# 16-row attentions of a four-layer kernel: negated row maxima turned by VectorE and placed by two small transfers, and maxima run 15 steps ahead

## The chip, the cores and the metric

One Trainium2 chip, one core. The metric is the device time of one execution in microseconds (us); before the change the median of three is 4501.39 us (4497.85 to 4503.6). TensorE (PE, with PEld for its weight loads), VectorE (DVE), ScalarE (ACT), GpSimd (POOL) and SyncE (SP) each work through their own instructions in order and wait for each other on semaphores.

## The reference, cut to what matters

The reference runs four layers, each an attention and a feed-forward part, over x of 8 sequences x 512 rows x 256 columns. The change touches one phase (L0x in the profile) that does three of these parts for all 8 sequences: the attention of layer 0, the gated attention of layer 0 and the attention of layer 1, all with 16 heads of 16 columns. That is 24 items (a part and a sequence each):

```python
qh = (q @ Wq.T + bq).reshape(N, L, h, d)          # h = 16 heads, d = 16
energy = jnp.einsum('nqhd,nkhd->nhqk', qh, kh)
attn = jax.nn.softmax(energy / math.sqrt(d), axis=-1)
out = jnp.einsum('nhql,nlhd->nhqd', attn, vh)
return out @ Wo.T + bo
```

Items 0 to 7 and 16 to 23 are of the kind "cross" (keys and values come from a context), items 8 to 15 of the kind "mixture" (queries are normalised per head, and the result is weighted by gates).

## The kernel before, in words

**Parts in bf16.** float32 queries and keys are cut into three bf16 parts each. GpSimd does this (`split`, lines 373 to 380, four operations of 1024 columns), SP sends the parts to DRAM (`parts_to_scratch`, L313) and loads them back as stacks of six 16-row parts (`stack_rows`, L289): `kstack` and `qstack`, 96 rows, 16 heads, 512 columns, two buffers each. An item needs 12 such loads of 256 KB, and the semaphore `stack_in` counts them.

**Two passes over the scores.** `for_maximum` (L760) multiplies 96 rows of the stacks for a (head, query tile) unit, queries on the partitions, into one of 3 banks of `ps_max`; VectorE takes the row maximum (`maximum`, L485). After 16 units, a group of 4 heads, `negated` (L492, L494) writes minus the maximum as two bf16 parts. `score` (L750) then computes the transposed scores with 104 rows: the 96 of the stacks and 8 more that add minus the maximum, and ScalarE takes the exponential (`exponentials`, L671). `values` (L774) multiplies the exponentials with the values.

**How the maxima get into the rows.** A fill `negmax` of TensorE (L827) multiplies the 128 x 8 block of each query tile with an identity, into the shared bank `ps_t`; ScalarE (`take_negmax`, L684) copies 8 rows x 512 columns for each of 4 heads into `qstack`. As all 4 heads get the same 8 rows, the key rows must pick out a head's own two: `own_key_rows` fills them once.

**Order of the work.** A round has 32 steps and belongs to item q. In step n TensorE does two scores of item q and two maximum units that lie `LEAD` = 12 steps ahead, thus of the next item from step 20 on. Unit 0 of an item waits for all 12 stack loads. After step n with n % 4 = 1 come the values. The other work of TensorE, the fills, goes one at a time through `ps_t` in steps written out by hand in `TURNS`: projections k, q, v, turned copies (xnT, hT, raw, qT), gates and output y, for the items q - 1 to q + 2. VectorE and ScalarE walk through the same steps. `negated` comes in steps 3, 11, 19 and 27, its fill in steps 5, 13, 21 and 29, and the first score of the group in steps 8, 16, 24 and 0.

**SP's queue.** In round q SP waits for the query parts of item q + 1 and stores them, loads kstack, and then

```python
if ahead.there and ahead.cross and ahead.later:
    if nxt.cross:
        sp.wait_ge(taken["v"], nxt.count(2, 2))
    context(ahead)
if nxt.there:
    sp.wait_ge(q_out, nxt.count(16, 16))
    stacked(nxt, 1, q_part, qstack)
```

`context` loads the 512 KB of keys and values of item q + 2 into the one buffer `kv_in`, which the fill v of item q + 1 (steps 9 and 10) reads last. This holds in 13 rounds, 0 to 5 and 15 to 21. The six loads of qstack stand behind it.

**GpSimd's gates.** `split` of the keys of item q + 2 waits for `negmax_ready` of the last group of item q, that of the queries (cross) for the first group of item q + 1.

Of the kernel before, what the change touches and what calls it, by code (L numbers as in the profile page):

```python
# [107 lines left out]
def rounds(steps):  # L108
# [5 lines left out]
    for number in range(-2, ITEMS + 1):  # L114
# [6 lines left out]
    "cross": [(4, "raw", 3), (5, "negmax", 1), (9, "v", 0), (10, "v", 1), (11, "hT", 0), (12, "hT", 1),  # L121
              (13, "negmax", 2), (14, "xnT", 0), (15, "raw", 0), (16, "y", 0), (17, "y", 1), (18, "xnT", 1),
              (19, "k", 0), (20, "k", 1), (21, "negmax", 3), (23, "raw", 1), (24, "q", 0), (26, "q", 1),
              (29, "negmax", 0), (31, "raw", 2)],
    "mixture": [(2, "v", 0), (3, "v", 1), (4, "raw", 3), (5, "negmax", 1), (7, "xnT", 0), (8, "xnT", 1),
                (9, "q", 0), (10, "q", 1), (11, "hT", 0), (12, "hT", 1), (13, "negmax", 2), (14, "k", 0),
                (15, "raw", 0), (16, "k", 1), (18, "gates", 0), (19, "qT", 0), (20, "qT", 1), (21, "negmax", 3),
                (22, "y", 0), (24, "y", 1), (25, "raw", 1), (29, "negmax", 0), (31, "raw", 2)],
# [9 lines left out]
def shift(what, c):  # L138

    if what in ("k", "xnT", "q", "qT"):  # L140
        return 2
    if what == "v" or (what, c) == ("negmax", 0):
        return 1
    if what in ("hT", "gates", "y") or (what, c) == ("raw", 3):
        return -1
    return 0


def softmax_attentions(nc, T, G, name, kind):
# [11 lines left out]
    LEAD = 12  # L161
# [3 lines left out]
    x_sb, ident, identb, own_rows = G["x"], G["ident"], G["identb"], G["own"]  # L165
    with Phase(nc, name) as ph:
# [21 lines left out]
        qstack = [ph.sb(f"qstack{b}", [ROWS + 8, HEADS, S], BF16) for b in range(2)]  # L188
        kstack = [ph.sb(f"kstack{b}", [ROWS + 8, HEADS, S], BF16) for b in range(2)]
        vpad = [ph.sb(f"vpad{b}", [P, TILES, HEADS * (HD + 1) + 15], F32) for b in range(2)]  # L190
        maxes = ph.sb("maxes", [P, TILES, HEADS], F32)
        negmax = ph.sb("negmax", [P, 2, TILES, 4, 2], BF16)
# [34 lines left out]
        vpad_ones, even_own_ready, odd_own_ready = (ph.sem("vpad_ones"), ph.sem("even_own_ready"),  # L227
                                                    ph.sem("odd_own_ready"))
# [51 lines left out]

        def own_key_rows(copy, stack):
            for g in range(4):
                for kt in range(TILES):
                    i = copy(stack[ROWS:ROWS + 8, 4 * g:4 * g + 4, kt * P:(kt + 1) * P], own_rows[ROWS:ROWS + 8])
            return i
# [62 lines left out]
        def _(pool):  # L348
# [84 lines left out]
            bias(Item(0))  # L433
# [2615 lines left out]
```

## Time and profile before

| | us |
|---|---|
| median of three executions | 4501.39 |
| the profiled execution, its time | 4504.13 |
| the profiled execution, its span | 4502.1 |
| first to last score of this phase | 73.9 to 1746.6 |

The times of the rows count from the span's start. Matmul durations in them contain a pipeline's fill and drain, so that two in a row overlap; the distance from start to start is what TensorE spends.

### The profile page before, as it was taken

What the parts mean: (1) busy time and instruction counts of PE and PEld (TensorE: products, weight loads), DVE (VectorE), ACT (ScalarE), POOL (GpSimd) and SP (SyncE); (2) the same over time, 40 slices, a digit from 0 to 9 for tenths busy, and PEclk for the clock granted to TensorE, in tenths of its full rate; (3) what the DMA queues carried; (4) which work ended last, traced back from release to release, by engine and by line L of the source; (5) the groups of instructions that cost most, each with busy time, mean ns of one, the idle gap of its engine ahead of it and who ended that gap; (6) DMA issues with size and microseconds to landing.
All of it is one profiled execution on the core that took longest, in us unless ns stands there. A gap on an engine that the chain in (4) does not pass through costs nothing. (4 is left out here: it accounts for less than half of the span.)

```text
span 4502.1 us, 66443 instructions
## 1 busy us (share of the span) xinstructions
PE 4233.5 (94%) x23716; PEld 2403.0 (53%) x23750; DVE 2976.9 (66%) x7431; ACT 2544.5 (57%) x6408; POOL 810.4 (18%) x550
## 2 busy tenths in 40 slices
PE   6999999999999996778989999999999998999999
PEld 2344344444343343567545666666666665555555
DVE  5767777777767776867675666676776766344333
ACT  3767666666667765633555776767676775111111
POOL 2322444443322311523010000000000000000000
PEclk8999999999999998999999999999999999999999
DMA  8456455444456451000100110010101102000000
GB/s 161 73 76 87 65 63 85 54 69 63 74 75 84 69 71 61 1 15 15 75 12 27 31 32 28 30 36 26 33 27 32 32 27 73 5 5 5 10 5 10
DMA packets 182844, 204.97 MB, mean 46 GB/s; under 512 B 44651, under 2 KB 165099, under 8 KB 180854
## 3 DMA queue, kind: packets, MB, share of 16 engines
q1 hardware_dynamic: 180886, 199.15, 24.1%
q8 instruction: 192, 3.15, 0.3%
q10 hardware_dynamic: 1632, 1.57, 0.3%
q14 instruction: 134, 1.10, 0.1%
HBM read 139.90 MB, written 60.78 MB: 45 GB/s over the span
## 5 line engine op out<-in xcount | busy, mean ns | idle before, releaser
L485 DVE TENSOR_REDUCE L0x_maxes<-L0x_ps_max 128x1 f32<-128x512 f32 x1536 | 976.5, 683 | 291.0 <-PE L0x_ps_max L760 289.3
L671 ACT ACTIVATE L0x_probs<-L0x_ps_sc 128x512 f32<-128x512 f32 x1536 | 822.7, 607 | 362.3 <-PE L0x_ps_sc L750 358.3
L760 PE MATMUL L0x_ps_max<-L0x_kstack,L0x_qstack 96*128 96x512 bf16 x1536 | 588.0, 384 | 22.7 <-DVE L0x_maxes L485 21.3
L2756 ACT ACTIVATE L3x_pexp<-L3x_ps,L3x_nmax 128x77 f32<-128x77 f32 (+2 forms) x1536 | 601.4, 433 | 0.0
L750 PE MATMUL L0x_ps_sc<-L0x_qstack,L0x_kstack 104*128 104x512 bf16 x1536 | 557.7, 384 | 11.5 <-ACT L0x_probs L671 11.0
L2638 DVE TENSOR_REDUCE L3x_nmax<-L3x_ps 128x2 f32<-128x154 f32 (+2 forms) x768 | 346.3, 506 | 242.1 <-PE L3x_ps L2869 239.7
L2764 ACT COPY L3x_pT<-L3x_ps 128x512 f32<-128x512 f32 x512 | 275.1, 593 | 225.8 <-PE L3x_ps L2877 225.4
L2256 ACT ACTIVATE L3f_act_g<-L3f_ps_gu 128x512 f32<-128x512 f32 x128 | 76.4, 597 | 542.2 <-PE L3f_ps_gu L2302 542.1
L774 PE MATMUL L0x_ps_out<-L0x_probs,L0x_vpad 128*32 128x512 f32 x3072 | 371.0, 601 | 1.1 <-ACT L0x_probs L671 1.1
L2654 DVE TENSOR_SCALAR L3x_pexp<-L3x_pexp,L3x_rsum 128x77 f32<-128x77 f32 (+2 forms) x1536 | 357.7, 306 | 6.8
L2756 ACT ACTIVATION_READ_ACCUMULATOR L3x_pexp<-L3x_ps,L3x_nmax 128x1 f32 x1536 | 359.4, 235 | 0.0
L2199 DVE TENSOR_TENSOR L3f_h<-L3f_act_g,L3f_ps_gu 128x512 f32<-128x512 f32 x128 | 88.0, 687 | 383.1 <-ACT L3f_act_g L2256 382.9
L760 PEld LDWEIGHTS L0x_ps_max<-L0x_kstack,L0x_qstack 96*128 96x128 bf16 x1536 | 151.0, 98 | 282.5 <-DVE L0x_maxes L485 167.5
L2895 PE MATMUL L3x_ps<-L3x_pT,L3x_v 128*64 128x128 f32 x4096 | 279.9, 279 | 0.7 <-ACT L3x_oT L2772 0.7
L2877 PEld LDWEIGHTS L3x_ps<-ident,L3x_pexp 128*128 128x128 f32 x2048 | 239.1, 141 | 73.4 <-issue 55.5
L2877 PE MATMUL L3x_ps<-ident,L3x_pexp 128*128 128x128 f32 x2048 | 266.1, 273 | 0.9 <-DVE L3x_pexp L2654 0.9
L750 PEld LDWEIGHTS L0x_ps_sc<-L0x_qstack,L0x_kstack 104*128 104x128 bf16 x1536 | 150.6, 98 | 211.7 <-ACT L0x_probs L671 81.1
L2599 POOL TENSOR_TENSOR L3x_v<-L3x_v,L3x_relv 128x256 f32<-128x256 f32 x32 | 23.4, 731 | 1294.7 <-ACT L3x_v L2739 1294.7
L2302 PE MATMUL L3f_ps_gu<-L3f_xnT,L3f_wg 128*128 128x512 f32 x512 | 243.0, 597 | 2.1 <-DMA L3f_wd<-in_L3f_wd 2.1
L2313 PE MATMUL L3f_ps_y<-L3f_wd,L3f_h 128*128 128x256 f32 x1024 | 242.4, 380 | 1.5 <-DVE x_res L2209 1.5
L2895 PEld LDWEIGHTS L3x_ps<-L3x_pT,L3x_v 128*64 128x64 f32 x4096 | 218.3, 136 | 43.4 <-issue 42.5
L2302 PE MATMUL L3f_ps_gu<-L3f_xnT,L3f_wu 128*128 128x512 f32 x512 | 240.6, 592 | 0.0
(377 smaller groups left out, 6841.4 us busy)
## 6 DMA issues: line engine op xcount, KB each, us to landing
L0x_kstack<-parts_scratch SPq DMA_DIRECT2D x141, 256.0 KB, 10.0
L0x_qstack<-parts_scratch SPq DMA_DIRECT2D x141, 256.0 KB, 14.5
parts_scratch<-L0x_kparts SPq DMA_DIRECT2D x24, 768.0 KB, 3.7
parts_scratch<-L0x_qparts SPq DMA_DIRECT2D x24, 768.0 KB, 5.0
rel_scratch<-L3x_rel_e SPq DMA_DIRECT2D x32, 408.0 KB, 2.4
L3x_rel_d<-prob_scratch SPq DMA_DIRECT2D x32, 408.0 KB, 3.1
L0x_kv_in<-in_ctxT SPq DMA_DIRECT2D x16, 512.0 KB, 4.5
L3x_rel_t<-rel_scratch SPq DMA_DIRECT2D x32, 154.0 KB, 2.4
```

Of the source, the lines that this page charges most:

```text
L485: V.tensor_reduce(maxes[:, t, head:head + 1], ps_max[:, q.count(64, unit) % BANKS, :], AX.X, ALU.max).then_inc(max_taken, 1)
L671: nc.scalar.activation(probs[:, step % SLOTS, j], ps_sc[:, at % BANKS, :], ACT.Exp, scale=HD ** -0.5).then_inc(probs_ready, 1)
L750: nc.tensor.matmul(ps_sc[:, at % BANKS, :], kstack[q.parity][:, head, kt * P:(kt + 1) * P], qstack[q.parity][:, head, :], start=True, stop ...
L760: nc.tensor.matmul(ps_max[:, at % BANKS, :], qstack[q.parity][0:ROWS, head, t * P:(t + 1) * P], kstack[q.parity][0:ROWS, head, :], start=T ...
L774: i = nc.tensor.matmul(ps_out[32 * j:32 * j + 32, :], vpad[q.parity][:, kt, (HD + 1) * head:(HD + 1) * head + 32], probs[:, q.count(STEPS, ...
L2302: i = nc.tensor.matmul(ps_gu[:, n % 2, k], w[:, ci, n * P:(n + 1) * P], xnT[:, ci, :], start=(ci == 0), stop=(ci == C - 1))
L2638: i = V.tensor_reduce(nmax[:, n % 4, s], ps[:, bank:bank + 2, a:b], AX.X, ALU.max, negate=True)
L2654: i = V.tensor_scalar(pexp[:, m % 4, e, a:b], pexp[:, m % 4, e, a:b], rsum[:, m % 4, s, e:e + 1], None, ALU.mult)
L2756: i = nc.scalar.activation(pexp[:, n % 4, e, a:b], ps[:, SB + 2 * (n % 2) + e, a:b], ACT.Exp, bias=nmax[:, n % 4, s, e:e + 1], accum_out=s ...
L2764: nc.scalar.copy(pT[:, m % 2, e], ps[:, TB + e]).then_inc(pt_ready, 1)
L2877: i = nc.tensor.transpose(ps[:, TB + e, kt * P:(kt + 1) * P], pexp[:, m % 4, e, kt * P:(kt + 1) * P], ident[:])
L2895: i = nc.tensor.matmul(ps[DIMH * e:DIMH * (e + 1), OB, at:at + P], v[g % 2][:, vt, h * DIMH:(h + 1) * DIMH], pT[:, m % 2, e, kt * P:(kt + ...
```

## The change

The fill `negmax`, its bank turns and ScalarE's copy go. VectorE lays the two bf16 parts of a group out as 32 columns (head, part, tile), turns them in 32 x 32 blocks into `negT`, ScalarE's queue sends `negT` to DRAM (`negmax_out`, step n % 8 = 1, 8 KB in rows of 64 B) and three steps later, once that has landed, loads them from there into two rows of `qstack`, each head its own (`negmax_in`, step n % 8 = 4, 8 rows of 1 KB). Score rows go from 104 to 98, the two key rows are plain ones set once by a memset, and `LEAD` goes from 12 to 15: `negated` now comes in steps 0, 8, 16 and 24, and unit 0 of the next item in step 17.

```diff
-    "cross": [(4, "raw", 3), (5, "negmax", 1), ... (13, "negmax", 2), ... (21, "negmax", 3), ... (29, "negmax", 0), (31, "raw", 2)],
+    "cross": [(4, "raw", 3), (9, "v", 0), ... (31, "raw", 2)],
...
-    LEAD = 12
+    NEG = 2
+    LEAD = 15
+    OUT_AT, IN_AT = 1, 4
...
-        negmax = ph.sb("negmax", [P, 2, TILES, 4, 2], BF16)
+        negmax = ph.sb("negmax", [P, 2, 4, NEG, TILES], BF16)
+        negT = ph.sb("negT", [P, 2, 32], BF16)
...
+            pool.wait_ge(biased, 1)
+            nc.gpsimd.memset(kstack[1][ROWS:ROWS + NEG], 1.0).then_inc(odd_ones_ready, 1)
+            pool.wait_ge(odd_ones_ready, 1)
...
+            V.memset(kstack[0][ROWS:ROWS + NEG], 1.0).then_inc(even_ones_ready, 1)
...
+                if group >= 2:
+                    dve.wait_ge(neg_turned, group - 1)
...
+                dve.wait_ge(negmax_ready, group + 1)
+                if group >= 2:
+                    dve.wait_ge(neg_out, 16 * (group - 1))
+                V.transpose(negT[:, g % 2, :], negmax[:, g % 2].rearrange("p h e t -> p (h e t)")
+                            ).then_inc(neg_turned, 1)
...
-            def take_negmax(q, g):
-
-                act.wait_ge(in_bank["negmax"], q.count(4, g + 1))
-                nc.scalar.copy(qstack[q.parity][ROWS:ROWS + 8, 4 * g:4 * g + 4, :],
-                               ps_t[ROWS:ROWS + 8, :].unsqueeze(1).broadcast_to([8, 4, S])
-                               ).then_inc(taken["negmax"], 1)
+            def negmax_out(q, g):
+
+                act.wait_ge(neg_turned, q.count(4, g + 1))
+                act.dma_start(T["neg_scratch"].rearrange("x (a r) -> a x r", a=4), negT[:, g % 2, :]
+                              ).then_inc(neg_out, 16)
+
+            def negmax_in(q, g):
+
+                act.wait_ge(neg_out, 16 * q.count(4, g + 1))
+                act.dma_start(qstack[q.parity][ROWS:ROWS + NEG, 4 * g:4 * g + 4, :],
+                              T["neg_scratch"].rearrange("(h e t) p -> e h (t p)", e=NEG, t=TILES)
+                              ).then_inc(neg_in, 16)
...
                     if q.there:
                         exponentials(q, n)
+                    if n % 8 in (OUT_AT, IN_AT):
+                        owner, g = (q, n // 8 + 1) if n < 24 else (q.plus(1), 0)
+                        if owner.there:
+                            (negmax_out if n % 8 == OUT_AT else negmax_in)(owner, g)
...
                 if n % 8 == 0 and j == 0:
-                    pe.wait_ge(taken["negmax"], q.count(4, g + 1))
+                    pe.wait_ge(neg_in, 16 * q.count(4, g + 1))
...
-                elif w == "negmax":
-                    pe.wait_ge(negmax_ready, q.count(4, c + 1))
-                    for t in range(TILES):
-                        i = nc.tensor.matmul(ps_t[ROWS:ROWS + 8, t * P:(t + 1) * P],
-                                             negmax[:, c % 2, t].rearrange("p h e -> p (h e)"), identb[:],
-                                             start=True, stop=True, tile_position=(0, ROWS))
...
+    T["neg_scratch"] = nc.dram_tensor("neg_scratch", (32, P), BF16, kind="Internal").ap()
```

## Rows read from the trace of the kernel before

**Rows 1.** The page: busy time, share of the span and instructions of each engine.
```profile
PE 4233.5 (94%) x23716; PEld 2403.0 (53%) x23750; DVE 2976.9 (66%) x7431; ACT 2544.5 (57%) x6408; POOL 810.4 (18%) x550
```

**Rows 2.** Busy time by stretch: start:end, length, engines, TensorE's clock, DMA share, GB/s.
```profile
74.00:1750.00 1676.00, 1595.30 (x8585) 674.29 (x8583) 1221.33 (x2469) 1128.44 (x1916) 553.33 (x277) 0.99 0.50 70
```

**Rows 3.** Timeline of TensorE around the fill of step 5, round 3.
```profile
284.12 0.38 PE L760 MATMUL L0x_ps_max<-L0x_kstack,L0x_qstack 96*128 96x512 bf16 x1
284.66 0.39 PE L827 MATMUL L0x_ps_t<-identb,L0x_negmax 128*8 128x128 bf16 x4 [0.16 <-DVE L0x_htok L513]
284.98 0.39 PE L750 MATMUL L0x_ps_sc<-L0x_qstack,L0x_kstack 104*128 104x512 bf16 x1
```

**Rows 4.** Groups of instructions, 0 to 2000 us: count, busy, mean ns, idle before.
```profile
L684 ACT CAST L0x_qstack<-L0x_ps_t 8x2048 bf16<-8x2048 f32 x96 | 178.4, 1858 | 15.0 <-PE L0x_ps_t L827 11.8
...
L827 PE MATMUL L0x_ps_t<-identb,L0x_negmax 128*8 128x128 bf16 x384 | 37.0, 218 | 18.5 <-DVE L0x_htok L513 8.6 <-DVE L0x_negmax L494 7.1 <-ACT L0x_qf L698 1.3
```

**Rows 5.** Timeline of SP's queue in round 3, which starts at 276.4 us.
```profile
298.41 0.36 SPq L296 DMA_DIRECT2D L0x_kv_in<-in_ctxT  x1
298.81 2.89 SPq L289 DMA_DIRECT2D L0x_qstack<-parts_scratch  x6
```

**Rows 6.** The six loads of qstack in round 3: their line, 298 to 303 us.
```profile
L289 SPq DMA_DIRECT2D L0x_qstack<-parts_scratch x6: 432/448/449, 298.8 to 301.3; - x6
...
DMA to landing us min/median/max: 6.4/10.9/15.3
```

**Rows 7.** Timeline of TensorE: first maximum of step 17, round 3.
```profile
313.15 0.38 PE L760 MATMUL L0x_ps_max<-L0x_kstack,L0x_qstack 96*128 96x512 bf16 x1
```

**Rows 8.** The same loads in round 15 (line, 1170 to 1175 us).
```profile
L289 SPq DMA_DIRECT2D L0x_qstack<-parts_scratch x6: 432/448/449, 1170.5 to 1173.0; - x6
...
DMA to landing us min/median/max: 6.3/10.6/14.6
```

**Rows 9.** Timeline of TensorE: first maximum of step 17, round 15.
```profile
1181.19 0.39 PE L760 MATMUL L0x_ps_max<-L0x_kstack,L0x_qstack 96*128 96x512 bf16 x1
```

**Rows 10.** Waits of SP's queue, 74 to 1700 us: total, times, longest.
```profile
SPq L296 <- DVE L0x_vpad L501: 188.3, 13, 14.7
```

**Rows 11.** Timeline of VectorE in step 21, round 9: part of the gates' chain.
```profile
751.98 1.97 DVE L577 SCALAR_TENSOR_TENSOR L0x_gtop<-L0x_gsw,L0x_gshare 128x4 f32<-128x4 f32 x1
753.98 0.16 DVE L579 TENSOR_TENSOR L0x_gscale<-L0x_gtop,L0x_gpart 128x4 f32<-128x4 f32 x1
```

**Rows 12.** Timeline of GpSimd at the same time.
```profile
745.64 1.90 POOL L373 TENSOR_TENSOR L0x_kparts<-L0x_kf,one 128x1024 bf16<-128x1024 f32 x1 [4.14 <-DVE L0x_negmax L494]
...
751.81 2.12 POOL L380 TENSOR_TENSOR L0x_kparts<-L0x_kf,L0x_kparts 128x1024 bf16<-128x1024 f32 x1
```

**Rows 13.** Timeline of TensorE after it, and the fill behind.
```profile
755.71 0.39 PE L760 MATMUL L0x_ps_max<-L0x_kstack,L0x_qstack 96*128 96x512 bf16 x1 [2.55 <-DVE L0x_maxes L485]
755.94 3.51 PE L795 MATMUL L0x_ps_t<-L0x_wo_mixture,L0x_hT 128*128 128x256 f32 x8
```

**Rows 14.** Busy time by stretch, behind TensorE's idle time.
```profile
756.10:759.50 3.40, 3.40 (x10) 2.40 (x9) 1.35 (x3) 0.00 (x0) 3.32 (x3) 0.51 0.32 108
```

**Rows 15.** The first instruction of `negated`: min/median/max ns.
```profile
L492 DVE TENSOR_SCALAR L0x_negmax<-L0x_maxes x96: 178/179/1257, 70.1 to 1730.8; 128x16 bf16<-128x16 f32 x96
```

**Rows 16.** DMA issues of small transfers: count, KB, us to landing.
```profile
L3f_wr<-in_L3f_wr SPq DMA_DIRECT2D x1, 8.0 KB, 1.6
...
bias_scratch<-L1f_bsplit SPq DMA_DIRECT2D x1, 7.5 KB, 4.9
```

**Rows 17.** Timeline of ScalarE: exponentials of steps 3 and 4, round 3.
```profile
282.73 2.24 ACT L671 ACTIVATE L0x_probs<-L0x_ps_sc 128x512 f32<-128x512 f32 x4
```

**Rows 18.** Timeline of TensorE: the first score of step 8, round 3.
```profile
289.74 0.38 PE L750 MATMUL L0x_ps_sc<-L0x_qstack,L0x_kstack 104*128 104x512 bf16 x1
```

**Rows 19.** Timeline of TensorE: the first maxima, and the first score.
```profile
58.52 0.81 PE L760 MATMUL L0x_ps_max<-L0x_kstack,L0x_qstack 96*128 96x512 bf16 x3
...
73.91 0.63 PE L750 MATMUL L0x_ps_sc<-L0x_qstack,L0x_kstack 104*128 104x512 bf16 x1
```

More of the change, by code:

```diff
@@ L120 @@
 TURNS = {
[L121 to L128, printed above, removed]
+    "cross": [(4, "raw", 3), (9, "v", 0), (10, "v", 1), (11, "hT", 0), (12, "hT", 1), (14, "xnT", 0), (15, "raw", 0), (16, "y", 0), (17, "y", 1), (18, "xnT", 1),
+              (19, "k", 0), (20, "k", 1), (23, "raw", 1), (24, "q", 0), (26, "q", 1), (31, "raw", 2)],
+    "mixture": [(2, "v", 0), (3, "v", 1), (4, "raw", 3), (7, "xnT", 0), (8, "xnT", 1),
[3 rows of a table added]
 }
@@ L141, in shift @@
         return 2
-    if what == "v" or (what, c) == ("negmax", 0):
+    if what == "v":
         return 1
@@ L164, in softmax_attentions @@
     PER = 4
-    x_sb, ident, identb, own_rows = G["x"], G["ident"], G["identb"], G["own"]
+    x_sb, ident = G["x"], G["ident"]
     with Phase(nc, name) as ph:
@@ L279, in weights_here @@
             engine.wait_ge(weights_in[LAYERS[q.layer]], n_weights[q.kind])
[L281 to L285, printed above, removed]
         def stack_rows(engine, q, here, part_of, stack, r):
@@ L490, in negated @@
                 own = maxes[:, :, 4 * g:4 * g + 4]
+                group = q.count(4, g)
                 dve.wait_ge(max_taken, q.count(64, 16 * g + 16))
-                V.tensor_scalar(negmax[:, g % 2, :, :, 0], own, -1.0, None, ALU.mult).then_inc(neg_step, 1)
+                if group >= 2:
+                    dve.wait_ge(neg_turned, group - 1)
+                V.tensor_scalar(negmax[:, g % 2, :, 0, :].rearrange("p h t -> p t h"), own, -1.0, None, ALU.mult).then_inc(neg_step, 1)
                 dve.wait_ge(neg_step, q.count(4, g + 1))
-                V.scalar_tensor_tensor(out=negmax[:, g % 2, :, :, 1], in0=own, scalar=-1.0,
-                                       in1=negmax[:, g % 2, :, :, 0], op0=ALU.mult,
+                V.scalar_tensor_tensor(out=negmax[:, g % 2, :, 1, :].rearrange("p h t -> p t h"), in0=own, scalar=-1.0,
+                                       in1=negmax[:, g % 2, :, 0, :].rearrange("p h t -> p t h"), op0=ALU.mult,
                                        op1=ALU.subtract).then_inc(negmax_ready, 1)
+                dve.wait_ge(negmax_ready, group + 1)
[3 more added lines that the diff above has]
+                            ).then_inc(neg_turned, 1)
             def take_v(q, half):
@@ L628, in steps @@
                         gate_scale(prev)
-                    if q.number == -1 and n == 16:
-                        own_key_rows(V.tensor_copy, kstack[0]).then_inc(even_own_ready, 1)
                     if not ahead.there:
```

17 lines of the change are left out of this document (7 added, 10 removed), and 3 rows, old and new, of the table TURNS.

## The prediction, made before the changed kernel ran

> **What bounds the kernel now.** I read the page first. TensorE is busy 94% of the span, VectorE 66% and ScalarE 57% [rows 1]. The phase that changes is the stretch from 74 to 1750 us, and there TensorE is busy 1595 of 1676 us at full clock, with VectorE and ScalarE at 1221 and 1128 [rows 2]. So 24 rounds take 69.8 us each on average, and what a removed instruction is worth is read from TensorE's line, instruction by instruction. A fill that goes gives back its own time and the wait in front of it; work that goes from ScalarE gives back only what TensorE waited for. The rest of the program is not touched, so the whole change of time must arise between the start and 1750 us.
>
> The profiled execution took 4504.1 us for a span of 4502.1, the median is 4501.4. I sum differences, which hold for either, and state the result against the median.
>
> **What goes from TensorE.** A round has four `negmax` fills. The one in step 5 of round 3 starts 0.54 us after the maximum in front of it, where scores and maxima follow each other in 0.22, and the next score comes 0.32 after it [rows 3]. Without the fill that score could follow the maximum at 0.22, so 0.64 us go. Read the same way the other three of this round give 0.65, 0.41 and 0.39 (the last is held by exponentials). Where the trace groups them, the 384 matmuls have 18.5 us of idle time before them [rows 4], mostly a wait for VectorE to free the bank. In mixture rounds the waits are longer and I get 2.0 to 2.9 us a round. ScalarE loses 96 copies of 1.86 us [rows 4]; hardly any score stands behind them, as the values of 1.8 us follow, so I count nothing for the 178 us. It gets two DMA issues a group instead, at 0.45 us each by SP's issues (2.89 us for six) [rows 5], which fit in the time of the copy that goes.
>
> Sum for the 9 full rounds 6 to 14 and the last two: 24 us gained. For the 13 others only the savings outside steps 10 to 17 count, for the reason that follows: 1.45 us x 13 = 19 us. Together 43 us.
>
> **What moves: the first maximum of the next item, from step 20 to step 17.** It waits for all 12 stack loads. In 13 rounds the six loads of qstack stand in SP's queue behind the load of `kv_in`, and that waits for the fill v of steps 9 and 10: SP waits for it 13 times, 188 us in all [rows 10]. In round 3 `kv_in` is issued at 298.4 and the loads right after, the last at 301.3 [rows 5]; that one lands 15.3 us later, at 316.6 [rows 6]. Before the change nobody waits for it, as unit 0 comes at step 20, near 322. Step 17's first maximum stands at 313.15 [rows 7]. Put there, unit 0 waits 3.4 us, and everything of TensorE waits behind it, because its queue is in order: the score beside it, the values, the fills. In round 15, whose steps 10 to 17 are shorter, the last load lands at 1173.0 + 14.6 = 1187.6 [rows 8] against 1181.2 [rows 9]: 6.4 us. By the same subtraction round 0 gives 4.9, round 16 6.7 and the nine others 2.6 to 3.3 (mean 2.9). The total is 9 x 2.9 + 3.4 + 4.9 + 6.4 + 6.7, about 47 us. The landing is tied to fill v. What is saved before step 10 moves both; what is saved between 10 and 17 only makes the wait longer. That is why I left it out above. Nothing else shortens the wait: the diff leaves SP's order alone.
>
> **TensorE's clock after such a wait.** In round 9 TensorE stands idle 2.55 us at step 23 and the fill behind takes 3.51 us [rows 13]; the granted clock is 0.51 for the 3.4 us after it, the lower level of 1.2 GHz [rows 14]. All five idle times of this length in the phase (rounds 9 to 13) are followed by it, and those rounds lose about 1.4 us more than the wait. The new wait is 3.4 us in round 3 plus the 0.65 saved in step 13, longer than these. Bounds: 0 and 13 x 1.4 = 18 us, more in rounds 15 and 16. I take 12, since part of the slow stretch can fall into the wait itself.
>
> **VectorE.** `negated` keeps its two operations of 0.18 us and gets a third and a wait. The transpose of 32 columns is not in the trace; the 16-column operations give 0.18 [rows 15], and I take 0.2 to 0.3 with its wait, between 0.1 and 0.5. Steps 8, 16 and 24 have a fill of 1.8 us beside them in cross rounds, and step 0 is followed by values; VectorE idles there, so this costs nothing. Without that cover it would be 24 x 4 x 0.3 = 29 us.
>
> **GpSimd against VectorE.** In round 9 a VectorE operation on 128 x 4 takes 1.97 us where its neighbour takes 0.16 [rows 11], and it ends with GpSimd's split operation, at 751.81 + 2.12 [rows 12]. The Trainium skill ("SBUF — State Buffer", section "SBUF: two separate sides") says that such a pair holds an exclusive lock for a whole instruction; the trace agrees with 1.97 against 0.16. The split of the keys had been released at 745.6 by `negmax_ready` of step 19 [rows 12]. Now that comes in step 16, about 6 us earlier, the split is over before this chain, and TensorE's wait of 2.55 us with its 1.4 us of clock would go: 4.0 us in each of 5 rounds, 20 us gained. But the earlier split then meets the gates' first operations in step 18 (up to 2 us, 5 rounds), and `negated` of step 24 meets the split of the queries in rounds 7 to 13, where a stalled `negated` has taken up to 1.26 us [rows 15] and two or three operations can be caught. I take 17 of the 20 as given back, bounds 20 gained to 10 lost.
>
> **The two transfers.** Out and in have no like in the trace. 8 KB read took 1.6 us, 7.5 KB written in short rows 4.9 [rows 16]; these are my bounds for each. ScalarE waits for the first in step 4, with 5.3 us between, and TensorE for the second in step 8. In round 3 the second can be issued after the exponentials that end at 285.0 [rows 17], at 285.4, and the score stands at 289.7 [rows 18], 0.6 earlier without the fill: 3.7 us. By the lower bound there is 2 us to spare, by the upper 1.2 missing. Queued behind a late ScalarE wait are the exponentials of step 5, and for them wait scores and values. I take 2.5 us each and no stall. The Trainium skill ("DMA: Bandwidth & Descriptors", section "Queues, rings and completion order") says that an engine switches between queues only after a whole packet. By that the transfers would each wait behind a share of a stack load, which in round 3 land (301.3 + 15.3 - 298.8 - 6.4) / 5 = 2.3 us apart, and the second would miss step 8 by about 1 us; no row before shows it.
>
> **Start and end.** The first maximum comes at 58.5 and the first score at 73.9 [rows 19], 12 steps of 1.28 us. Three more steps cost 3.8 us; maxima can start 1 us earlier, and the end has three steps with less work. Memsets lie in idle time. Net 4 us lost, 1 to 7.
>
> **Sum.** -43 (fills) + 47 (stack wait) + 12 (clock) - 3 (GpSimd) + 4 (start) = +17 us: 4501.4 + 17 = 4518 us.
>
> **Rivals.** (1) *The gates' chain comes free and the clock holds*: -43 + 47 - 20 + 0 + 4 = -12, with the start at its low end -15: 4486 to 4490 us. It decides if VectorE's operations in step 21 of rounds 9 to 13 are back at 0.16 us and nothing new is caught. For it speaks the release three steps earlier, against it that GpSimd's work has to lie somewhere under VectorE's. Chance 0.17. (2) *The round trip is late as well*: 1 us in step 8 in about 15 rounds and the clock low in all 13, 17 + 15 + 6 = +38: 4539 us, up to 4560. Chance 0.17. (3) *The change does what it says and the two large terms cancel*, without loss of clock: within 9 us of before. Chance 0.17. The forecast, 4511 to 4530, has 0.49.
>
> What a measurement of this kernel tells from no change is about 0.2%, 9 us. Faster than that is rival 1, 0.17; within it rival 3, 0.17; slower the forecast and rival 2, 0.66. The range that leaves out no more than 2 in 10 takes in the bounds of the clock, the chain and the late transfer: 4484 to 4556.
>
> **What would show it.** Right: in 13 rounds a wait of TensorE before L760 of 3 to 7 us, ended by the DMA of `qstack`, and a granted clock near 0.5 behind it; rounds 1 to 5, measured from first score to first score, 1.5 to 3 us longer and rounds 7 and 8 shorter by 2. Wrong: stacks landed before step 17, because the loads or fill v come earlier; TensorE waiting for the small transfer in steps 0, 8, 16 or 24; VectorE's chain at full speed in rounds 9 to 13; or the four fills giving back far more than 2 us a round.

## The result, and the profile after

The changed kernel takes 4818.09 us (median; 4813.53 to 4828.87) where before takes 4502.5 on the same chip: ratio 1.0702, 95% interval 1.0688 to 1.0715. I had forecast 4518 us and a range up to 4556. The direction was right, the size was not: 316 us in place of 17.

The page of the changed kernel: busy time by engine, TensorE's granted clock in 40 slices, and the groups of scores, maxima and exponentials with the idle time before them.

```profile
PE 4303.0 (89%) x23332; PEld 2425.0 (50%) x23366; DVE 3015.5 (62%) x7512; ACT 2359.0 (49%) x6296; POOL 815.2 (17%) x551
...
PEclk7999999899898999989999899999999999999999
...
L676 ACT ACTIVATE L0x_probs<-L0x_ps_sc 128x512 f32<-128x512 f32 x1536 | 823.0, 613 | 815.2 <-PE L0x_ps_sc L760 679.3
L760 PE MATMUL L0x_ps_sc<-L0x_qstack,L0x_kstack 98*128 98x512 bf16 x1536 | 589.3, 402 | 276.6 <-DMA L0x_qstack<-neg_scratch 188.7
L770 PE MATMUL L0x_ps_max<-L0x_kstack,L0x_qstack 96*128 96x512 bf16 x1536 | 620.0, 405 | 42.6 <-DMA L0x_qstack<-parts_scratch 22.3
```

ScalarE has lost its copies (2544.5 to 2359.0 us busy, [rows 1]), as planned, and TensorE has 384 matmuls fewer. Yet TensorE is busy longer, 4303.0 us against 4233.5: the matmuls that are left run at a lower clock. The third line of groups names the place: 188.7 us of TensorE's idle time ends with the landing of the second small transfer, in front of a score. The wait that I had counted on, for the stacks in front of L770, is only 22.3 us, and 16.4 of them lie at the start, before the first score.

The waits between 83 and 2073 us (engine, instruction, what it waited for: us, times, longest):

```profile
PE L0x_ps_sc L760 <- DMA L0x_qstack<-neg_scratch: 188.7, 35, 11.3
ACT L0x_probs L676 <- DMA neg_scratch<-L0x_negT: 131.3, 24, 10.2
PE L0x_ps_sc L760 <- ACT L0x_probs L676: 86.8, 50, 7.6
PE L0x_ps_max L770 <- DMA L0x_qstack<-parts_scratch: 5.9, 2, 3.5
```

Both transfers are late. The first holds ScalarE, and behind ScalarE's exponentials TensorE waits 86.8 us. The second holds TensorE itself. Round 3 shows how. First SP's queue, then ScalarE, then TensorE at the scores of steps 6 and 8 (start, duration, and in brackets the idle time before and what ended it):

```profile
329.38 0.38 SPq L309 DMA_DIRECT2D parts_scratch<-L0x_qparts  x1
329.85 4.02 SPq L285 DMA_DIRECT2D L0x_kstack<-parts_scratch  x6
```
```profile
331.88 0.54 ACTq L689 DMA_DIRECT2D neg_scratch<-L0x_negT  x1
...
341.94 0.23 ACTq L695 DMA_DIRECT2D L0x_qstack<-neg_scratch  x1
342.22 3.04 ACT L676 ACTIVATE L0x_probs<-L0x_ps_sc 128x512 f32<-128x512 f32 x6 [5.11 <-DMA neg_scratch<-L0x_negT]
```
```profile
342.87 0.39 PE L760 MATMUL L0x_ps_sc<-L0x_qstack,L0x_kstack 98*128 98x512 bf16 x1 [2.91 <-ACT L0x_probs L676]
...
348.17 0.61 PE L760 MATMUL L0x_ps_sc<-L0x_qstack,L0x_kstack 98*128 98x512 bf16 x1 [3.29 <-DMA L0x_qstack<-neg_scratch]
...
348.99 0.63 PE L760 MATMUL L0x_ps_sc<-L0x_qstack,L0x_kstack 98*128 98x512 bf16 x1
```

The first transfer is issued at 331.88, when three kstack loads are in flight (issued, and not yet landed); ScalarE goes on at 341.94, 10.1 us later. The second is issued there, with three loads left, and lands at 348.1, 6.2 us later. I had allowed 2.5 us each. Behind it the score takes 0.61 to 0.63 us instead of 0.38, and the granted clock of the next 4 us is 0.50, the lower level of 1.2 GHz (start:end, length, engines, clock, DMA share, GB/s):

```profile
348.50:352.50 4.00, 4.00 (x11) 2.75 (x10) 2.34 (x10) 1.19 (x2) 0.50 (x2) 0.50 0.00 0
```

Eight steps later it repeats with the second transfer alone. It is issued right behind the six qstack loads, and TensorE gets it 13.8 us later:

```profile
359.63 2.89 SPq L285 DMA_DIRECT2D L0x_qstack<-parts_scratch  x6
```
```profile
362.47 0.23 ACTq L695 DMA_DIRECT2D L0x_qstack<-neg_scratch  x1
```
```profile
376.31 0.61 PE L760 MATMUL L0x_ps_sc<-L0x_qstack,L0x_kstack 98*128 98x512 bf16 x1 [5.66 <-DMA L0x_qstack<-neg_scratch]
```

The loads themselves have kept their pace. The line of the six, from 359 to 363 us:

```profile
DMA to landing us min/median/max: 5.8/10.4/14.9
```

The last of them, issued at 362.1, lands at 377.0; the small one, issued 0.4 us behind it, has landed by 376.3. The stamps of the two semaphores in the trace show this for all 192 transfers. The 133 that find no load in flight take mostly 1.9 and 1.5 us (at most 4.4). Of the 59 that find some, 49 land within 1.1 us of the last load that was in flight at their issue, and 8 more within 2.4 us; for example 13.79 us against 14.51 with six in flight, and in round 7 18.16 against 17.44 with eight. The other two land 6 us ahead of the last of nine. So a small transfer waits for nearly the whole backlog (the loads issued before it that have not landed), not for a share of it.

It is the data that are late, and not only the signal of their landing. The trace counts packets by queue: q1 carries SP's transfers, q10 ScalarE's. From the issue of the first transfer at 331.88 to 339.40 us:

```profile
q1 hardware_dynamic: 1099, 1.07, 110.3%
```

and from 339.40 to 340.15 us:

```profile
q1 hardware_dynamic: 75, 0.07, 99.5%
q10 hardware_dynamic: 132, 0.01, 33.5%
```

No packet of ScalarE's queue moves for 7.5 us, then all 132 within 0.7; the semaphore follows at 341.92, 1.8 us after the last. For the 59 transfers together, 466 of their 638 us lie between the issue and the first packet (1.7 to 11.8 us each), and the last packet is 0.8 to 2.3 us ahead of the semaphore. The transfers that meet nothing have 1.2 and 0.9 us to the first packet, and 0.5 and 0.4 from the last to the semaphore (medians of the first and the second).

### The profile page after: what moved, and what is told of

The parts are those of the page before. It is cut to its first block and busy times, and to the rows that moved or that the text cites. A ratio compares the mean times of both kernels' runs of the same rounds, so it can differ in the third digit from the quotient of the medians.

```text
span 4827.1 us, 65930 instructions
## 1 busy us (share of the span) xinstructions
PE 4303.0 (89%) x23332; PEld 2425.0 (50%) x23366; DVE 3015.5 (62%) x7512; ACT 2359.0 (49%) x6296; POOL 815.2 (17%) x551
## 5 line engine op out<-in xcount | busy, mean ns | idle before, releaser
L760 PE MATMUL L0x_ps_sc<-L0x_qstack,L0x_kstack 98*128 98x512 bf16 x1536 | 589.3, 402 | 276.6 <-DMA L0x_qstack<-neg_scratch 188.7
L770 PE MATMUL L0x_ps_max<-L0x_kstack,L0x_qstack 96*128 96x512 bf16 x1536 | 620.0, 405 | 42.6 <-DMA L0x_qstack<-parts_scratch 22.3
L760 PEld LDWEIGHTS L0x_ps_sc<-L0x_qstack,L0x_kstack 98*128 98x128 bf16 x1536 | 154.6, 101 | 515.6 <-DMA L0x_qstack<-neg_scratch 206.4
L770 PEld LDWEIGHTS L0x_ps_max<-L0x_kstack,L0x_qstack 96*128 96x128 bf16 x1536 | 155.6, 101 | 342.4 <-DVE L0x_maxes L485 185.4
L2881 PEld LDWEIGHTS L3x_ps<-ident,L3x_pexp 128*128 128x128 f32 x2048 | 239.1, 141 | 73.4 <-issue 55.5
## 6 DMA issues: line engine op xcount, KB each, us to landing
L0x_kstack<-parts_scratch SPq DMA_DIRECT2D x141, 256.0 KB, 10.1
```

The costliest lines, as they stand in the source:

```text
L760: nc.tensor.matmul(ps_sc[:, at % BANKS, :], kstack[q.parity][:, head, kt * P:(kt + 1) * P], qstack[q.parity][:, head, :], start=True, stop ...
L770: nc.tensor.matmul(ps_max[:, at % BANKS, :], qstack[q.parity][0:ROWS, head, t * P:(t + 1) * P], kstack[q.parity][0:ROWS, head, :], start=T ...
L2881: i = nc.tensor.transpose(ps[:, TB + e, kt * P:(kt + 1) * P], pexp[:, m % 4, e, kt * P:(kt + 1) * P], ident[:])
```

## The experiments

All ratios are to the kernel before on the same chip, with 95% intervals. The table has the lengths of the rounds, from first score to first score, read off each trace (us). "New order" has the qstack loads ahead of `kv_in` in SP's queue; "two in flight" allows two stack loads at a time. The traces of the three kernels that start as before have their first score at 73.9 to 77.2, so a difference of 3 us there says nothing.

| kernel | median | ratio | first score | rounds 1 to 5, mean | rounds 9 to 13, mean |
|---|---|---|---|---|---|
| before | 4502.5 | | 73.9 | 68.2 | 75.7 |
| changed | 4818.1 | 1.0702 | 83.6 | 81.8 | 86.0 |
| no round trip | 4544.1 | 1.0088 | 85.4 | 71.3 | 71.2 |
| before, no fills | 4481.3 | 0.9946 | 76.2 | 67.1 | 74.3 |
| before, LEAD 15 | 4558.4 | 1.0122 | 82.8 | 73.0 | 71.0 |
| no round trip, new order | 4472.2 | 0.9927 | 86.1 | 66.5 | 71.2 |
| two in flight, new order | 4505.3 | 1.0006 | 85.5 | 69.3 | 71.2 |
| two in flight, new order, loads held for the first transfer, start as in the last row | 4492.7 | 0.9974 | 78.0 | 67.1 | 71.2 |
| before, LEAD 15, new order, early fills at the start | 4477.8 | 0.9942 | 78.9 | 67.5 | 71.0 |

**Is it the round trip? Without it.** Both transfers and the waits for them are left out.

```diff
-                    pe.wait_ge(neg_in, 16 * q.count(4, g + 1))
+                    pe.wait_ge(neg_turned, q.count(4, g + 1))
...
-                            (negmax_out if n % 8 == OUT_AT else negmax_in)(owner, g)
```

> The changed kernel without its round trip: neither small transfer is issued and nobody waits for one, the first score of a group waits for VectorE's transpose only, and the two score rows stay zero (so the maxima are not subtracted). All else, the 15 steps of lead included, stays. Theory A (the round trip's lateness is the whole excess over my sum): the 316 us go, the time comes to what my sum gave for everything else, 4500 to 4530 us, and a stack wait of 3 to 7 us at step 17 in 13 rounds is back, since rounds are short again. Rival B (the lead of 15, the stack wait, VectorE's longer chain or the clock carry the loss): over 4650 us.

Measured: 4544.07 us, 1.0088 (1.0071 to 1.0105). 274 us go with the round trip, and 38 of the change's loss remain, where my sum had 17: the time lies 14 us above A's range, so the round trip is most of the excess and not the whole. The stack wait is back, as A said:

```profile
PE L0x_ps_max L766 <- DMA L0x_qstack<-parts_scratch: 55.4, 13, 7.1
```

The phase with and without the trip (first score to last, columns as above) splits the loss:

```profile
83.60:2072.30 1988.70, 1660.79 (x8183) 695.61 (x8181) 1254.32 (x2557) 953.34 (x1819) 551.25 (x276) 0.90 0.43 60
```
```profile
85.40:1786.90 1701.50, 1583.95 (x8182) 650.73 (x8180) 1246.55 (x2557) 947.21 (x1819) 549.54 (x275) 0.98 0.49 69
```

The phase is 287 us longer with the trip: 210 are idle time of TensorE (327.9 against 117.5) and 77 the same matmuls at a lower clock (busy 1660.8 against 1584.0, clock 0.90 against 0.98). The 210 are about 189 of waits for the second transfer and 77 more for ScalarE's exponentials (86.8 against 10.3), less 50 of stack wait that the late rounds hide. These two traces are the longest of the one kernel's executions and the shortest of the other's, so they lie 290 us apart where the medians lie 274.

**Slow transfers, or transfers in a queue? The loads made small.** Loads of items 2 to 23 bring 2 heads of 16; the other heads are computed from old rows.

```diff
-            engine.dma_start(stack[q.parity][HD * r:HD * r + HD, :, :],
+            heads = 2 if q.number >= 2 else HEADS
+            engine.dma_start(stack[q.parity][HD * r:HD * r + HD, 0:heads, :],
```

> The changed kernel with the stack loads of items 2 to 23 cut from 16 heads to 2 (32 KB each in place of 256; the other heads are computed with old rows); count, order and waits stay. Theory A (a small transfer is late because it stands behind the stack loads in the DMA engines): both small transfers take 1.5 to 2.5 us in every group, nobody waits for them, and without the stack wait as well the time is 4440 to 4500 us. Rival B (the transfers are slow by themselves: rows of 64 B, few engines, two hops through DRAM, or ScalarE issues them late): waits for them stay in steps 4, 8 and 16 and the time stays over 4700 us.

Measured: 4479.57 us, 0.9943 (0.9928 to 0.9957). The transfers are the same, and in rounds 1 to 23 no wait of TensorE ends with one of them (ScalarE has one, of 0.5 us). Round 0, whose loads are still whole, takes 83.4 us, round 1 takes 66.5. Theory A holds and B falls.

**One hop in place of two.** Four transfers from `negT` straight into `qstack`, all issued in step 1.

```diff
-                act.dma_start(T["neg_scratch"].rearrange("x (a r) -> a x r", a=4), negT[:, g % 2, :]
-                              ).then_inc(neg_out, 16)
+                for a in range(4):
+                    act.dma_start(qstack[q.parity][ROWS:ROWS + NEG, 4 * g:4 * g + 4, :]
+                                  .rearrange("e h (t a r) -> e (h t) a r", t=TILES, a=4)[:, :, a],
+                                  negT[32 * a:32 * a + 32, g % 2, :]).then_inc(neg_in, 16)
```

> The changed kernel with one hop in place of two: four transfers of 32 rows of 64 B go from negT straight into the two rows of qstack, all issued in step 1 of a group, and ScalarE waits for none of them; TensorE waits in step 8 as before. Theory A: under the stack loads a hop takes the 6 to 14 us that each of the two took, but it has the 15 us between steps 1 and 8 to itself, so that waits before the first score mostly vanish; four issues at 0.45 us cost ScalarE nothing that scores stand behind. 4510 to 4600 us. Rival B (each hop's time is set by small rows between SBUF and SBUF or by the count of issues): a hop takes over 15 us or ScalarE becomes late, over 4700 us.

Measured: 4776.3 us, 1.0600 (1.0584 to 1.0616), a miss for A and inside B's range. In round 3:

```profile
322.78 2.60 ACTq L690 DMA_DIRECT2D L0x_qstack<-L0x_negT  x4
```
```profile
339.36 0.61 PE L755 MATMUL L0x_ps_sc<-L0x_qstack,L0x_kstack 98*128 98x512 bf16 x1 [6.00 <-DMA L0x_qstack<-L0x_negT]
```

The fourth is issued at 324.76, now behind all six kstack loads, and lands 14.6 us later, when the last of them does (14.4). I had let a hop take 6 to 14 us and forgotten that four issues of 0.65 us move the last one behind the whole backlog. A's 15 us were not there either: from the first issue to where the score would have stood (339.36 - 6.00) there are 10.6 us. The wait in front of the first score is 167.8 us in all, and the stack wait of 55.5 us in 13 rounds comes on top. The four issues, 2.6 us, also stand ahead of ScalarE's exponentials: for those TensorE waits 40.3 us, and 10.3 in the run without the trip. That part is B's, but it is the smaller one: with a short backlog the same four issues, and 40.8 us of that wait, run in 4509.75 us (below).

**The loads moved away.** The kstack loads wait for the second small transfer, the qstack loads follow at once and kv_in comes last.

```diff
+                    if q.there:
+                        sp.wait_ge(neg_in, 16 * q.count(4, 2))
...
                     stacked(nxt, 0, k_part, kstack)
+                    sp.wait_ge(q_out, nxt.count(16, 16))
+                    stacked(nxt, 1, q_part, qstack)
```

> The changed kernel with SP's queue in another order: the kstack loads wait until the small transfer of step 4 has landed, the qstack loads follow at once, and kv_in, which waits for fill v, comes behind them. So no stack load is in flight in steps 1 to 4 or 12. Theory A: the transfers of steps 1, 4, 9, 12 land in 1.5 to 3 us, the stack wait at step 17 goes too (the last load lands some 20 us after step 4, before step 15), and the time is 4440 to 4500 us. Rival B (other traffic or the transfers themselves are late): waits of 3 us and more stay in steps 4, 8 or 16, over 4650 us. Rival C: the loads, held for 8 us, land after step 17, and the wait only moves: 4520 to 4600 us.

Measured: 4668.03 us, 1.0358 (1.0342 to 1.0373), inside B's range, but not for B's reason: the waits have left the group whose loads are held and stand at the next one. TensorE waits 2.8 us for the second transfer and not at all for the stacks, and the 12 loads now stand in one backlog from 10 us of the round on. The transfer of step 9 meets it, with nine loads in flight, and takes 18.18 us; ScalarE waits for it, and TensorE for ScalarE:

```profile
ACT L0x_probs L677 <- DMA neg_scratch<-L0x_negT: 214.1, 24, 11.8
PE L0x_ps_sc L761 <- ACT L0x_probs L677: 154.5, 52, 9.4
```

**A short backlog.** SP issues load r only when load r - 2 has landed.

```diff
+                        if q.later:
+                            sp.wait_ge(pair_in[r % 2], q.count(96, 16 * (r // 2 + 3 * here)))
                         stack_rows(sp, q, here, part_of, stack, r)
```

> The changed kernel with at most two stack loads in flight: SP issues load r only when load r - 2 has landed (two semaphores, even and odd loads). Order and size of everything stay. Theory A, sharpened by the runs before (a small transfer lands when the loads that were in flight at its issue have landed, some 2.3 us each): none takes over 6.5 us, TensorE's waits for qstack<-neg_scratch fall from 189 us to under 50, and the stack wait at step 17, 55 us in 13 rounds without the round trip, is back: 4550 to 4610 us. Rival B (it is the load of the engines as such, not the depth of what stands ahead): transfers issued beside loads still take 10 us and more, over 4700 us.

Measured: 4592.45 us, 1.0194 (1.0177 to 1.0211), inside A, though 16 of the 192 small transfers take over A's 6.5 us, the longest 8.5. The same bytes move at the same pace (loads land 2.3 us apart, median, in this run and in the changed kernel), only the depth ahead of a transfer changes:

```profile
ACT L0x_probs L679 <- DMA neg_scratch<-L0x_negT: 39.0, 15, 4.0
PE L0x_ps_sc L763 <- DMA L0x_qstack<-neg_scratch: 22.7, 14, 2.3
```

This is the run that parts depth from load: 188.7 us of TensorE's wait became 22.7. The stack wait is there 13 times, 61 us (three of them ended by the DMA of `qstack`, ten shown as "issue").

**With the new order as well.** The qstack loads ahead of kv_in.

> As the run with two loads in flight, and the qstack loads stand ahead of kv_in in SP's queue. Theory A: round trip in time, the 12 loads land by 33 us of the round, before step 17 at 37 us, so the stack wait of 55 us and the low clock behind it go too: 4475 to 4520 us. Rival C (two in flight starve the loads: over 3 us each, the last lands after step 17): 4540 to 4600 us.

Measured: 4505.29 us, 1.0006 (0.9996 to 1.0015), inside A. The change now costs nothing, and gains nothing.

**With one hop too.**

> As the last, with the one hop of four transfers in place of out and in. Theory A: each transfer lands within 6.5 us, the hop has 15 us, ScalarE never waits, and what a late 'out' costs there in step 4 goes: 4465 to 4505 us, at or below the run with the round trip. Rival D (96 x 4 issues of 0.65 us on ScalarE, where two stood, make the exponentials late): 10 to 60 us above it.

Measured: 4509.75 us, 1.0009 (0.9999 to 1.0018): 4 us above, with an interval that takes it in. Rounds 1 to 5 are shorter (68.1 us on average against 69.3), and rounds 6, 7 and the last give it back (77.8, 74.9 and 57.1 us against 72.9, 69.7 and 51.3). ScalarE's four issues keep 40.8 us of TensorE's waits for exponentials alive. The time lies 5 us above A's range and short of D's 10 us over the other run: neither is clear.

**The parts of the change, one by one.** First the gain alone: the kernel before without its fills and copies (score rows stay zero).

```diff
-(5, "negmax", 1), (13, "negmax", 2), (21, "negmax", 3), (29, "negmax", 0)
...
-                    pe.wait_ge(taken["negmax"], q.count(4, g + 1))
+                    pe.wait_ge(negmax_ready, q.count(4, g + 1))
```

> The kernel before without the four negmax fills and ScalarE's copies (the eight score rows stay zero, so the maxima are not subtracted); LEAD stays 12. It prices the gain alone. By my reading of the fills: 24 us in rounds 6 to 14 and the last two, and some 2.1 us in each of the 13 others, whose steps 10 to 17 save as well when no stack wait follows: 51 us, about 4454 us (4445 to 4465). Rival: the gaps beside the fills are taken over by the next wait of TensorE: under 30 us gained, over 4475.

Measured: 4481.28 us, 0.9946 (0.9931 to 0.9961): 24 us gained of the 51 that my reading gives for this run, as the rival had it. TensorE's waits for VectorE's maxima before and in this run:

```profile
PE L0x_ps_max L760 <- DVE L0x_maxes L485: 18.4, 22, 2.6
```
```profile
PE L0x_ps_max L761 <- DVE L0x_maxes L486: 37.5, 54, 2.8
```

A fill stood partly in time that TensorE would otherwise spend waiting for the next free bank. A cross round gets 1.1 us shorter (67.1 against 68.2), and I had read 2.1.

**The lead alone**, in the kernel before: `LEAD = 15`.

> The kernel before with LEAD 15 in place of 12 and nothing else: fills and copies stay in steps 5, 13, 21 and 29. It prices the move of the first maximum alone. By my sum: a stack wait at step 17 of 47 us in all (no saving ahead of it, so some 5 less), 12 of clock behind it, 3 less from GpSimd, 4 at the start: +55 to +65 us, 4560 to 4572. If the fills hid part of the wait, or the clock holds: +30 to +45 us. Rival: no stack wait, within 9 us of before; then the 15 steps of lead are free and the excess of the run without the round trip has another cause.

Measured: 4558.42 us, 1.0122 (1.0107 to 1.0137), 54 us lost, just under the expected 55 to 65. That the sum is near is luck, as two terms were off and cancel: the 13 rounds with the stack wait (54.2 us of waits in all) are 73 us longer in its trace, where I had 59; rounds 9 to 13 are 24 us shorter, where I had 3; the first score is 9 us later, where I had 4.

**The stack wait alone**: no round trip, and the qstack loads ahead of kv_in.

> The changed kernel without its round trip (score rows stay zero, so the maxima are not subtracted), and with the qstack loads ahead of kv_in in SP's queue. Against the run without the round trip alone (4544 us) it prices the stack wait of step 17: 55 us of waits in the trace, and 5 to 15 us of low clock behind them. 4474 to 4490 us. Rival: the loads land no earlier, since kstack fills the time before: over 4520.

Measured: 4472.24 us, 0.9927 (0.9914 to 0.9941), 2 us below the expected range. Against 4544.07 the stack wait and its clock cost 72 us. It is also where this design ends with a round trip that is always in time, but for the start.

**The start.** Two in flight, new order, and in the round ahead of item 0 xnT and k of item 1 in steps 15 and 16.

```diff
+            early = {("xnT", 1): 15, ("k", 0): 16, ("k", 1): 16} if q.number == -1 else {}
```

> As the run with two loads in flight and the new order (4505 us), and in the round ahead of item 0 the fills xnT and k of item 1 come in steps 15 and 16 in place of 18 to 20. With LEAD 15 unit 0 stands in step 17 and waits for the stacks until 60.3 us, and those three fills, which TensorE did in that wait before the change, stand behind it; GpSimd's split of the keys starts at 69.7 where it was 59.5. Theory: the first score comes 4 to 7 us sooner, 4498 to 4501 us. Rival: the start is bound by the splits and loads of item 0 and the maxima themselves: within 2 us.

Measured: 4509.2 us, 1.0011 (1.0002 to 1.0020), a miss: no gain, and the first score comes at 88.4, no earlier than the 85.5 without the edit. The new order had put kv_in behind item 0's qstack loads, and the fill k, now in front, waits for it:

```profile
59.68 3.75 PE L802 MATMUL L0x_ps_t<-L0x_kv_in,L0x_wk_cross 128*128 128x512 f32 x4 [12.97 <-DMA L0x_kv_in<-in_ctxT]
```

**Held for both transfers.** Two kstack loads, then a wait for `neg_in`, and `IN_AT = 3`.

> As the last, and two things more for the group of steps 1 to 8, where the two-in-flight run still had waits of 22 us (TensorE) and 35 us (ScalarE): only two kstack loads are issued ahead of it, the rest wait until its second small transfer has landed, and that one is issued in step 3 in place of 4. Theory A: its waits go in 13 rounds, and 10 loads of 2.3 us from 9 us of the round on still land before step 17: 4480 to 4492 us. Rival C: the loads end after step 17 and the stack wait is back: 4505 to 4530.

Measured: 4535.4 us, 1.0072 (1.0059 to 1.0084), 5 us above C's range. The stack wait of C is back only three times, 7.8 us in all, and A's waits have not gone. In round 3 the first transfer still takes 7 us, behind the store of the query parts and two loads, and a wait one step earlier holds ScalarE longer: 51.9 us in all against 35.4 with two in flight.

**Held for the first transfer only**, and kv_in in its old place at the start.

```diff
+                    if q.there:
+                        sp.wait_ge(neg_out, 16 * q.count(4, 2))
```

> The changed kernel with two loads in flight, and the kstack loads wait until the first small transfer of step 1 has landed (by 6 us of the round, with only the store of the query parts ahead of it; the run before held them for the second one too, and its ScalarE then waited 52 us). qstack ahead of kv_in in full rounds only, fills xnT and k of item 1 in steps 15 and 16 at the start, kv_in there ahead of qstack as in the kernel before. Theory A: out of step 1 takes 3 us in place of 7, both waits of steps 4 and 8 go in 13 rounds, loads still land by 36 us; first score at 79 to 81 us: 4470 to 4485 us. Rival C: the loads end after step 17 or the start does not move: 4490 to 4510.

Measured: 4492.72 us, 0.9974 (0.9964 to 0.9984). The time is C's, and both happened. The waits for small transfers are gone, as A has it:

```profile
PEld L0x_ps_sc L770 <- DMA L0x_qstack<-neg_scratch: 3.4, 7, 0.6
ACT L0x_probs L686 <- DMA neg_scratch<-L0x_negT: 0.6, 1, 0.6
```

Rounds 1 to 5 take 67.1 us, and the first score comes at 78.0. What is left stands in rounds 0 and 14 to 16 (77 to 79 us each for the three, 71 to 75 without the trip): there the loads now end after step 17, and three waits of TensorE for them, 13.9 us, fall into these rounds.

**GpSimd's release alone**, in the kernel before.

```diff
-                        pool.wait_ge(negmax_ready, q.count(4, 4))
+                        pool.wait_ge(max_taken, q.count(64, 58))
```

> The kernel before with one line changed: GpSimd's split of the keys is released by unit 57 of the maxima (step 16) and no longer by the negated maxima of step 19. If GpSimd's later release is what held VectorE's gates' chain in rounds 9 to 13 (75.5 us each, 71.2 in every run with 15 steps of lead), those rounds come to 71 to 72 and the time to 4480 to 4486 us. If it is the lead of the maxima itself (VectorE has done more ahead), it stays within 6 us of before.

Measured: 4514.37 us, 1.0022 (1.0013 to 1.0031), outside both: 11 us slower, where the first theory had some 20 gained and the second at most 6 either way. 3 of the 11 lie before the first score (77.2), which this edit does not touch. The chain of [rows 11] is at full speed, and the stall has moved to `negated` of step 19, where the split now lies. Rounds 9 to 13 gain 1.1 us on average, rounds 6 to 8 lose 4. Round 9 on VectorE, GpSimd and TensorE:

```profile
761.78 1.63 DVE L492 TENSOR_SCALAR L0x_negmax<-L0x_maxes 128x16 bf16<-128x16 f32 x1
```
```profile
761.49 1.89 POOL L378 TENSOR_TENSOR L0x_kparts<-L0x_kf,one 128x1024 bf16<-128x1024 f32 x1
```
```profile
763.78 0.38 PE L827 MATMUL L0x_ps_t<-identb,L0x_negmax 128*8 128x128 bf16 x4 [1.75 <-DVE L0x_negmax L494]
```

**The schedule without the transfers.** The kernel before, its fills and copies kept, with LEAD 15, the new order in full rounds and the early fills at the start.

> The kernel before with its fills and copies, with LEAD 15, the qstack loads ahead of kv_in in full rounds, and xnT and k of item 1 in steps 15 and 16 at the start. It has every other part of the change, so it says what the turned and transferred maxima themselves are worth beside the fills. Expected from LEAD 15 alone (4558 us): 55 to 70 us of stack wait and clock less, 4 at the start less: 4482 to 4500 us, some 20 us (the fills' price) above the run with the round trip in time.

Measured: 4477.82 us, 0.9942 (0.9929 to 0.9954), faster than both kernels, 4 us below the expected range, and 15 us under the best one with transfers, where I had expected it 20 above. Its page:

```profile
PE 4233.6 (95%) x23750; PEld 2398.4 (54%) x23750; DVE 2972.6 (66%) x7431; ACT 2543.2 (57%) x6408; POOL 810.3 (18%) x550
```

## Why the prediction was wrong

**The step that failed** is the one on the two transfers: "I take 2.5 us each and no stall", with bounds of 1.6 and 4.9 us from [rows 16]. The runs put 274 us in its place: behind one to nine loads the transfers took 4 to 18 us. The number was right for transfers that meet nothing, 1.9 and 1.5 us, and the loads that stand in the same steps were in my rows [rows 5, 6]: in round 3 before, loads issued over 2.5 us land over 11. I used these landings for the stack wait and not for what stands behind them on the DMA engines. The upper bound should have been the backlog: 15 us. My rival 2 named the place and priced it at 1 us a round, and TensorE waiting for the small transfer in steps 0, 8, 16 or 24 stood among my signs of being wrong.

One of my two bounds showed the effect already. The read of 1.6 us met nothing, but the write of 4.9 us was issued behind three loads of weights, and the last of these is this one (SP's queue, then size and time to landing):

```profile
1765.66 1.08 SPq L1079 DMA_DIRECT2D L1f_wpr<-in_L1f_wpr  x1
1768.75 0.38 SPq L1081 DMA_DIRECT2D bias_scratch<-L1f_bsplit  x1
```
```profile
L1f_wpr<-in_L1f_wpr SPq DMA_DIRECT2D x1, 1024.0 KB, 7.7
```

The load lands at 1773.4 and the small write at 1773.7. I read the 4.9 us as the price of short rows; the first transfer takes 1.9 us alone, in rows of 64 B, which makes the backlog the likelier price; no run tried that write by itself. Both stand in one queue there, so this row alone could not tell that another engine's queue suffers as well.

I had weighed the Trainium skill ("DMA: Bandwidth & Descriptors", section "Queues, rings and completion order") there: an engine takes turns between queues at whole packets, from which I estimated a wait of one share, 2.3 us. The direction was right and the size was not: the second transfer of step 12 took 13.8 us behind six loads. Nor does the trace show turns at packets: in the 7.5 us above, 1099 packets of SP's queue began and none of ScalarE's. The same section says that the semaphore write lands only after every earlier write of that engine, across its queues. That would fit the 1.8 us from the last packet to the semaphore, against 0.5 alone; it does not explain the 7.5 us before the first packet, and why ScalarE's packets begin so late no run here tells.

**The rest of the sum** was 17 us and measured 38, and the errors in its terms partly cancel. One by one:

- Fills: -43 expected (-51 where no stack wait follows), -24 measured there. I counted the gap beside a fill as saved; about half of it became a wait for VectorE's maxima.
- Stack wait and clock: 47 + 12 = 59 expected, 72 measured without the round trip (55 of waits in 13 rounds, the rest clock). Mechanism, count and place were right. In the changed kernel itself the wait nearly vanished, since the rounds were late before step 17.
- GpSimd: -3 expected. With the lead alone rounds 9 to 13 went from 75.7 to 71.0, so 24 us; my rival 1 had this right. Fills and GpSimd share some of it: together they are -42 us in the phase (1630.6 us in the run with no trip and the new order, 1672.7 before), and -46 in my sum. In the changed kernel the split ends at 904.34 and the chain of step 21 follows at full speed:

```profile
904.98 0.16 DVE L585 SCALAR_TENSOR_TENSOR L0x_gtop<-L0x_gsw,L0x_gshare 128x4 f32<-128x4 f32 x1
```

  I had taken 17 of 20 back, for a split that meets other VectorE work. With the release alone just that happens (4514 us). With the lead, `negated` has left step 19 too, and the split of the keys meets neither. The other meeting that I had feared, `negated` of step 24 against the split of the queries, does happen in rounds 9 to 13 of the changed kernel:

```profile
912.16 1.96 DVE L497 SCALAR_TENSOR_TENSOR L0x_negmax<-L0x_maxes,L0x_negmax 128x16 bf16<-128x16 f32 x1
```

  As far as these rounds tell it costs next to nothing: without the round trip these rounds have it too and take 71.2 us, and in the kernel before with LEAD 15, where the longest such operation is 0.46 us in these rounds, they take 71.0. My 17 us had a price for a stall for which TensorE hardly waits.
- Start: 4 expected, about 8 measured. The first score comes at 82.3 to 86.1 (mean 84.0) in the ten kernels that start with the changed one's order of fills, at 73.9 to 77.2 (mean 75.8) in the three that start as before. Unit 0 in step 17 stands ahead of three fills of item 1 that TensorE did before while it waited for the stacks:

```profile
57.98 1.03 PE L770 MATMUL L0x_ps_max<-L0x_kstack,L0x_qstack 96*128 96x512 bf16 x2 [16.39 <-DMA L0x_qstack<-parts_scratch]
58.81 1.06 PE L792 MATMUL L0x_ps_t<-ident,L0x_xn 128*128 128x128 f32 x4
...
60.54 3.65 PE L797 MATMUL L0x_ps_t<-L0x_kv_in,L0x_wk_cross 128*128 128x512 f32 x4
...
64.97 1.98 PE L797 MATMUL L0x_ps_t<-L0x_kv_in,L0x_wk_cross 128*128 128x512 f32 x4 [0.34 <-ACT L0x_kf L704]
```

  With them back in front, and kv_in in its place, it comes at 78 to 79.

That makes -42 (fills and GpSimd together) + 72 + 8 = +38, as the run without the round trip has. The three are read from the same runs, so this is a split of the 38 and no second proof of it.

**VectorE's transpose**, costed at nothing, takes 0.21 us (96 times) and costs nothing that shows: with no trip and the new order rounds 1 to 5 take 66.5 us, less than the 67.1 of before without fills.

**The change itself** does not pay in any form tried here: on nearly the same schedule the fills give 4477.82 us and the transfers 4492.72. A cross round is 0.4 us shorter with the transfers; rounds 14 to 16 lose 17 us, since the loads, kept two in flight and held for the first transfer, have no room there. With no transfers and no limit on the loads it is 4472.24, with a first score 7 us later (86.1 against 78.9): some 6 to 13 us is the most that a round trip at no cost could gain over the fills, an estimate from these two runs.

## What to carry to other kernels

Price a small transfer by what is in flight on the DMA engines when it is issued, also from another engine's queue, and not by its bytes. When a row of the trace is to be a bound, look at what was in flight around it. If a latency-bound transfer must share with bulk loads, bound the backlog (two loads in flight kept their pace of 2.3 us each here) and let it be issued first. Before a step is moved earlier in an in-order queue, list what it now stands in front of: here the wait for the stacks passed three fills at the start. And when a removed instruction had a gap beside it, ask which engine's pace made the gap; it comes back in front of the next instruction.

## What was not expected of the hardware

Two engines' DMA queues do not shield each other: a transfer of 8 KB on ScalarE's queue took 18.2 us behind eight loads of SP's queue and 1.9 us without them. And the long waits of round 3 were each followed, at once or 1 us later, by matmuls of 0.61 to 0.63 us that take 0.38 otherwise (granted clock 0.50): over the phase that is 77 us of the loss, over a quarter of it.
